# Last residual groups, three statistics groups and the gathered copies of the first phase moved into the next step's first slot

## The reference, cut to what matters

```python
x = x + L0_conv(_ln_c(x), ...)       # clustering mixer, below
t = t + L0_ffn(_ln_t(t), ...)        # per token, 96 -> 384 -> 96, values rounded to fp8 e5m2 / f16
x = x + L1_conv(_ln_c(x), ...)       # depthwise 3x3, 1x5, 5x1, then 1x1, times x
t = t + L1_ffn(_ln_t(t), ...)
```

```python
centers = pool(feat)                                  # 4 centres, means over sub-quadrants
sim  = sigmoid(beta + alpha * cos(centers, feat))     # 4 numbers per token and head
sim  = sim * (one-hot of the first maximum)           # ties go to the first centre
agg  = (sim @ value + value_centers) / (sum(sim) + 1) # gather
out  = agg^T @ sim ;  y = proj(out)                   # spread back, residual added
```

## Time and profile before

| | |
|---|---|
| median of 3 runs | 3742.16 us |
| the profiled execution, its time | 3745.27 us |
| the same, span of its trace | 3743.4 us |
| DVE busy | 3187.9 us (85%) |
| PE busy | 2901.5 us (78%) |
| ACT busy | 2795.3 us (75%) |
| POOL busy | 1723.0 us (46%) |
| `phase_a` | from 0 to about 2055 us |

### The profile page before, as it was taken

One profiled execution on the slowest core, in us unless ns is written; L12 is line 12 of the kernel. 1 busy time (PEld: TensorE's weight loads), 2 busy tenths in 40 slices (PEclk: granted clock), 3 DMA queues, 4 the chain that ended last, 5 costly groups with the idle time before them and its releaser, 6 DMA issues. The chain is left out here.

```text
span 3743.4 us, 65658 instructions
## 1 busy us (share of the span) xinstructions
PE 2901.5 (78%) x20710; PEld 1901.6 (51%) x20710; DVE 3187.9 (85%) x8131; ACT 2795.3 (75%) x6274; POOL 1723.0 (46%) x2404
## 2 busy tenths in 40 slices
PE   5777777777777777677766899996878888887877
PEld 5565556555565656565643344442444444444443
DVE  4888888888888888888886799998888889889887
ACT  2577777777777777777778455553999999999998
POOL 3777777777777777777764000000222222222221
PEclk7788888888889888988887899998999999999999
DMA  3232323232323232323222888896666666666661
GB/s 66 52 79 76 86 74 89 69 86 69 86 69 86 69 86 69 86 69 85 69 60 75 222 236 237 238 295 178 183 175 175 195 174 178 191 178 174 189 189 57
DMA packets 696169, 478.77 MB, mean 128 GB/s; under 512 B 407217, under 2 KB 674422, under 8 KB 683830
## 3 DMA queue, kind: packets, MB, share of 16 engines
q1 hardware_dynamic: 695830, 474.58, 48.0%
HBM read 272.09 MB, written 201.92 MB: 127 GB/s over the span
## 5 line engine op out<-in xcount | busy, mean ns | idle before, releaser
L1881 POOL TENSOR_SCALAR C_var<-C_st 128x16 f32<-128x16 f32 x64 | 16.6, 259 | 1385.1 <-DVE C_st L178 1385.1
L1455 DVE SCALAR_TENSOR_TENSOR B_y<-B_mid,B_coefs,B_y 128x512 f32<-128x512 f32 x768 | 509.0, 742 | 3.2 <-ACT B_y L1420 3.2
L1386 PE MATMUL B_ps_row<-B_z,B_band 128*128 128x512 f32 x1152 | 497.6, 594 | 13.5 <-DMA B_band<-edge_scratch 13.5
L378 DVE TENSOR_SCALAR A_hq<-A_h,A_b 128x512 f16<-128x512 f16 x768 | 293.8, 418 | 236.4 <-ACT A_h L370 230.1
L370 ACT ACTIVATE A_h<-A_hid 128x512 f16<-128x512 f32 x768 | 427.1, 592 | 64.4 <-PE A_hid L357 61.4
L178 DVE BATCH_NORM_STATS2 A_st<-A_xT 128x6 f32<-128x192 f32 x1536 | 443.1, 349 | 26.2 <-ACT A_xT L852 13.0
L370 ACT ACTIVATE C_h<-C_hid 128x512 f16<-128x512 f32 x768 | 426.3, 592 | 16.7 <-PE C_hid L357 9.1
L1495 ACT ACTIVATE C_q<-C_xT,C_shift,C_rstd 128x96 fp8e5<-128x96 f32 x1024 | 391.5, 456 | 31.4 <-POOL C_shift L1888 31.4
L167 POOL TENSOR_TENSOR A_rstd<-A_var,A_expo 128x16 f32<-128x16 f32 x128 | 374.7, 2927 | 10.7
L885 ACT ACTIVATE A_xc<-A_xT,A_shift,A_rstd 128x96 f32<-128x96 f32 x1024 | 379.2, 456 | 0.0
L1386 PEld LDWEIGHTS B_ps_row<-B_z,B_band 128*128 128x128 f32 x1152 | 218.2, 190 | 291.5 <-issue 285.8
(11 more groups left out here) (165 smaller groups left out, 6985.2 us busy)
## 6 DMA issues: line engine op xcount, KB each, us to landing
A_xq<-in_x SPq DMA_DIRECT2D x32, 1536.0 KB, 8.9
x_scratch<-A_xT SPq DMA_DIRECT2D x64, 768.0 KB, 3.2
x_scratch<-A_x3h SPq DMA_DIRECT2D x64, 768.0 KB, 5.4
B_z<-x_scratch SPq DMA_DIRECT2D x96, 512.0 KB
y_scratch<-B_y SPq DMA_DIRECT2D x96, 512.0 KB, 3.6
C_x3q<-x_scratch SPq DMA_DIRECT2D x32, 1536.0 KB, 9.0
C_xT<-x_scratch SPq DMA_DIRECT2D x64, 768.0 KB, 15.5
C_y3q<-y_scratch SPq DMA_DIRECT2D x31, 1536.0 KB, 15.4
```

What stands on the lines that cost most here:

```text
L378: r = dve.tensor_scalar(self.hq[:, b, s], self.h16[:, b, s], self.w["b1"][:, j:j + 1], 0.0, ALU.add, ALU.max)
L1386: m = pe.matmul(bank(c, h), band[c.buf(NB)][:, d, :], z[c.buf(NB)][:, half(h), d:d + W], start=(d == 0), stop=(d == 2))
L1455: dve.scalar_tensor_tensor(y, mid[c.buf(2)][:, half(h), t:t + W], coefs[:, c.n, 3 + t:4 + t], y, ALU.mult, ALU.add).then_inc(ev["sums"], 1)
```

## The change

- `OUT_AT` keeps groups 0 to 5 in slots 3, 4, 5; groups 6 and 7 (`OUT_LATE`) go to slot 0 of the next step, where the block is i itself. POOL's `ln2(·, 1)` goes with them: it now stands near the head of the next step's POOL queue, as `ln2(i, 1)`.
- `bn1` of q4 has its own tables: groups 0, 1 in slot 7, 2, 3, 4 in slot 8, and 5, 6, 7 in slot 0 of the next step (`BN1_AT`, `BN1_LATE`). `fwd` stays. The residual groups' statistics are issued before `bn1`, and `similarity` before both.
- `gather_out` goes from slot 8 to slot 0 of the next step, behind the hidden work. `own_heads` goes to the start of slot 2, `values` to the end of slot 1.
- `turn_sim` goes from slots 5 and 7 to 6 and 8; the centres' chain (`SIDE_AT` to `CN2_AT`) one slot later, `CW_AT` stays 8.
- PE issues the late `out(i, i, k)` in slot 0 behind both `big` groups and ahead of `sum_rows`. The list of bank uses follows, so the uses four entries apart are others: `agg` now comes four after `fwd` of group 5, and `out(6)` four after `agg`.
- POOL's queue is reordered: see the end of the diff.
- `similarity` writes its masks into a wider `eq` (9 floats per token and head) and no longer copies mask 0; `projected` is one `scalar_tensor_tensor` with a constant block mask instead of four `tensor_scalar`.

In the diff, the order of calls that is changed stands first for PE, then for DVE (from `ff.dve_hidden` on), last for POOL (`body`).

```diff
-OUT_AT = {3: (0, 1), 4: (2, 3), 5: (4, 5), 6: (6, 7)}
+OUT_AT, OUT_LATE = {3: (0, 1), 4: (2, 3), 5: (4, 5)}, {0: (6, 7)}
+BN1_AT, BN1_LATE = {7: (0, 1), 8: (2, 3, 4)}, {0: (5, 6, 7)}
-SIMT_AT = {5: 0, 7: 1}
-SIDE_AT, STD_AT, MEAN_AT, CF_AT, CN2_AT, CW_AT = 2, 2, 3, 4, 5, 8
-AGG_AT, SUM_AT, VAL_AT, PA_AT = 8, 0, 1, 2
+SIMT_AT = {6: 0, 8: 1}
+SIDE_AT, STD_AT, MEAN_AT, CF_AT, CN2_AT, CW_AT = 3, 3, 4, 5, 6, 8
+AGG_AT, GATHER_AT, SUM_AT, VAL_AT, HEADS_AT, PA_AT = 8, 0, 0, 1, 2, 2
...
             if s == AGG_AT:
-                front_uses.append(("agg", 0, 2, "gathered", 0))
+                front_uses.append(("agg", 0, 2, "gathered", 1))
...
+                    for k in OUT_LATE.get(s, ()):
+                        if i.real:
+                            out(i, i, k)
...
-                e = eq[:, u, :]
+                e = eq[:, u, 0:M]
...
-                dve.tensor_copy(taken[:, u, 0], e[:, :, 0]).then_inc(ev["tie"], 1)
...
-                for t in range(TPC):
-                    g = slice(32 * t, 32 * t + 32)
-                    m = dve.tensor_scalar(pabd[g, t * C:(t + 1) * C], s_pa[g, 0:C], rden[g, :], None, ALU.mult)
-                m.then_inc(ev["pabd"], 1)
+                dve.scalar_tensor_tensor(pabd[:].rearrange("p (t c) -> p t c", c=C),
+                                         s_pa[:, 0:C].unsqueeze(1).to_broadcast([P, TPC, C]), rden[:],
+                                         own_block.unsqueeze(2).to_broadcast([P, TPC, C]),
+                                         ALU.mult, ALU.mult).then_inc(ev["pabd"], 1)
...
                         ff.dve_hidden(dve, i, s)
+                    if q1.real and s == GATHER_AT:
+                        gather_out(q1)
                     for c in BIG_AT.get(s, ()):
                         if q2.real:
                             norms(q2, c)
...
+                    for k in OUT_LATE.get(s, ()):
+                        if i.real:
+                            x1(i, k)
                     for k in OUT_AT.get(s, ()):
                         if q1.real:
                             x1(q1, k)
-                    for k in FWD_AT.get(s, ()):
-                        if q4.real:
-                            bn(q4, k, "xT", "bn1", st1)
+                    if q2.real and s in SIM_AT:
+                        similarity(q2, SIM_AT[s])
+                    for k in OUT_LATE.get(s, ()):
+                        if i.real:
+                            bn(i, k, "x1", "bn2", ff.st)
                     for k in OUT_AT.get(s, ()):
                         if q1.real:
                             bn(q1, k, "x1", "bn2", ff.st)
+                    for k in BN1_AT.get(s, ()):
+                        if q4.real:
+                            bn(q4, k, "xT", "bn1", st1)
+                    for k in BN1_LATE.get(s, ()):
+                        if q3.real:
+                            bn(q3, k, "xT", "bn1", st1)
...
             def body(i):
                 q1, q2, q3, q4, p = i + 1, i + 2, i + 3, i + 4, i - 1
+                if p.real:
+                    ln3(p, 1)
+                if i.real:
+                    ln2(i, 1)
+                    ff.pool_norm(pool, i, 2)
                 if q3.real:
                     ln1(q3, 1)
                     r_by_side(q3, 1)
...
+                if q2.real:
+                    inverse_norms(q2, 0)
+
+                    pool.wait_ge(ev["rn"], ev.at("rn", q2, 0))
                 if i.real:
-                    ff.pool_norm(pool, i, 2)
...
+                    ff.pool_norm(pool, i, 3)
+                if q2.real:
+                    inverse_norms(q2, 1)
+
+                    pool.wait_ge(ev["rn"], ev.at("rn", q2, 1))
                 if i.real:
                     ln3(i, 0)
                 if q2.real:
                     scaled_sim(q2, 0)
                 if q1.real:
                     ln2(q1, 0)
+                    ff.pool_norm(pool, q1, 0)
                 if q3.real:
                     centres(q3)
-                if q1.real:
-                    ff.pool_norm(pool, q1, 0)
                 if q2.real:
                     scaled_sim(q2, 1)
                 if q1.real:
-                    ln2(q1, 1)
                     ff.pool_norm(pool, q1, 1)
```

More of the change, by code:

```diff
@@ L53 @@
 K_QUARTERS = K_ROWS + HM
-K_W = K_QUARTERS + M
+K_BLOCK = K_QUARTERS + M
+K_W = K_BLOCK + TPC
 class Events:
@@ L449, in phase_a @@
             back_uses += [("c", k, 0, "cout", k) for k in C_AT.get(s, ())]
-            if s == VAL_AT:
-                front_uses.append(("val", 0, 1, "aT4", 0))
             front_uses += [("big", c, 2, "big", c) for c in BIG_AT.get(s, ())]
+            front_uses += [("out", k, 0, "x1", k) for k in OUT_LATE.get(s, ())]
             front_uses += [("out", k, 1, "x1", k) for k in OUT_AT.get(s, ())]
@@ L471, in phase_a @@
                     c16=1, cw=1, cwc=1, big=NK, n2=NK, n2c=2, seed=2, rn_s=22, rn=2, guarded=2, cos=2, sig=2, mx=2, eq=2,
-                    tie=6, only=2, sim=2, simr=2, simT=2, side=1, sided=1, pool=1, agg=1, gathered=2, sum=1, summed=1, val=1,
+                    tie=2 * (M - 2), only=2, sim=2, simr=2, simT=2, side=1, sided=1, pool=1, agg=1, gathered=2, sum=1, summed=1, val=1,
                     rden=1, aT4=1, pa=1, pabd=1, bn3=NK,
@@ L763, in centre, with out @@
                 pe.matmul(out, lhs, rhs, start=True, stop=True).then_inc(ev[stage], 1)
-            def out(i, k):
-                q = i + 1
+            def out(i, q, k):
                 if k == 0:
@@ L806, in body @@
                         ff.pe_y(pe, i, s - 1)
+                    for k in OUT_LATE.get(s, ()):
+                        if i.real:
+                            out(i, i, k)
                     for k in OUT_AT.get(s, ()):
                         if q1.real:
-                            out(i, k)
+                            out(i, q1, k)
                     for k in FWD_AT.get(s, ()):
@@ L814, in body @@
                         sum_rows(i)
+                    if q1.real and s == VAL_AT:
+                        values(i)
                     if q1.real and s == PA_AT:
@@ L1115, in body @@
                 for s in range(FFN_SLOTS):
-                    if q1.real and s == VAL_AT:
+                    if q1.real and s == HEADS_AT:
                         own_heads(q1)
@@ L1139, in body @@
                             bn(q1, k, "x1", "bn2", ff.st)
+                    for k in BN1_AT.get(s, ()):
[4 more added lines that the diff above has]
+                            bn(q3, k, "xT", "bn1", st1)
                     if q1.real and s == PA_AT:
                         projected(q1)
-                    if q2.real and s in SIM_AT:
-                        similarity(q2, SIM_AT[s])
-                    if q2.real and s == AGG_AT:
-                        gather_out(q2)
                     if q1.real and s == SUM_AT:
@@ L1255, in body @@
                     r_by_side(q3, 1)
+                if q2.real:
+                    inverse_norms(q2, 0)
+                    pool.wait_ge(ev["rn"], ev.at("rn", q2, 0))
                 if i.real:
-                    ff.pool_norm(pool, i, 2)
-                if p.real:
-                    ln3(p, 1)
-                for h in range(2):
-                    if q2.real:
-                        inverse_norms(q2, h)
-                        pool.wait_ge(ev["rn"], ev.at("rn", q2, h))
-                    if i.real and h == 0:
-                        ff.pool_norm(pool, i, 3)
+                    ff.pool_norm(pool, i, 3)
+                if q2.real:
+                    inverse_norms(q2, 1)
+                    pool.wait_ge(ev["rn"], ev.at("rn", q2, 1))
                 if i.real:
@@ L1935 @@
         consts[32 * t:32 * t + M, K_QUARTERS:K_QUARTERS + M] = np.eye(M, dtype=np.float32) / np.float32(2 * CH)
+    for t in range(TPC):
+        consts[32 * t:32 * t + 32, K_BLOCK + t] = 1
     consts[0:C, K_CEN:K_CEN + C] = np.eye(C, dtype=np.float32) - np.float32(1 / C)
```

22 lines of the change are left out of this document (12 added, 10 removed).

## The result

| | before | after |
|---|---|---|
| median of 4 runs | 3742.43 us (3741.0 to 3745.09) | 3851.23 us (3850.41 to 3853.87) |
| span of the profiled execution | 3743.4 us | 3849.4 us |
| DVE busy | 3187.9 us | 3250.5 us |
| PE busy, mean clock | 2901.5 us, 0.90 | 3012.7 us, 0.87 |

The change makes the kernel slower: ratio 1.0289, 95% interval 1.0276 to 1.0302. The forecast was 3762 us with a range to 3806; the sign was right, the size was not.

A forecast was written before the change was run, and what follows sets the result against it. A chain that changes engines sets the step, no engine being full: 23.1 + 28.7 + 10.6 = 62.4 us against 61.43, +25 over 28 steps, -5 after. +20 on 3745.3 gives 3765, median 3762 us, range 3695 to 3806.

The forecast's parts named there:

- T to C: From DVE's first hidden work in slot 0 to its `cosines(0)` in slot 3: 23.1 us against 19.3, through POOL's queue.
- C to h: From DVE's `cosines(0)` to the end of slot 7's hidden work: 28.7 us against 33.01, DVE taken as bound.
- h to T: From DVE's slot 7 hidden work ending to the next step's first: 10.6 us against 9.0, gather behind ACT's copy.
- 28 steps: The steady steps of `phase_a`, each +0.9 us longer: +25 us in all.
- the rest: Pipeline fill 0; steps 29 to 31, with less on POOL and more room on DVE, -5 us.
- Rival A: PE at the low clock for the late `out`, `bn2` 1.5 us later: +42, 3804 us, chance 0.17.
- The rule on the clock: PE idling is followed by 1.2 GHz: two `out` groups take 2.93 us, not 1.46; the sum used the full level.
- Rival B: The gather stays hidden, 9.0 us from slot 7's hidden work to the next step: 60.7 a step, 3717 us, chance 0.20.
- C (no wait at `cosines(0)`): DVE reaches `cosines(0)` 19.4 us into the step without waiting for POOL: 58.6 us a step, 3657 us, chance 0.08.

The follow-up runs named there:

- the experiment with the two savings: The kernel before with only the cheaper `similarity` and the fused `projected`, nothing moved: 3747.05 us, ratio 1.0008.
- both edits: The changed kernel with `turn_sim(1)` back in slot 7 and POOL's `ln1(q3, 1)` and `r_by_side` behind `inverse_norms(q2, 0)`: 3755.03 us, ratio 1.0025.
- the fastest: The changed kernel with `turn_sim(1)` in slot 7, `ln1(q3, 1)` behind `inverse_norms(q2, 0)`, and `gather_out` ahead of slot 0's hidden work: 3719.02 us, ratio 0.9936.

## Why the prediction was right in sign and wrong in size

Its own terms, in us, against what most steps of the profiled execution show:

| | predicted | measured |
|---|---|---|
| T to C | 23.1 | 23.10 (24.5 at the low clock) |
| C to h | 28.7 | 30.0 |
| h to T | 10.6 | 11.75 (10.5 when the low clock is elsewhere) |
| 28 steps | +25 | +93 |
| the rest: fill, last steps, later phases | -5 | +13 |

**T to C was right, with its parts.** `out(6)` started at T + 4.0 (said: about 3.95) behind 1.67 us of idling (said 1.5); POOL took the late statistics at T + 7.3 (said 7.3), and `cosines(0)` waited 3.4 us (said 3.7) for a POOL queue of 15.8 us. The kernel with POOL's order changed shows it as the cause: without 3.8 us of that queue T to C is 20.0.

**C to h is the first step that failed: "28.7 us" subtracted removed work from a stretch in which the rest was taken as fixed.** It measured 30.0. These differences make up the missing 1.3 us. The three chunks of slot 3 took 2.58 us, 1.44 in the kernel before: +1.1. One L383 took 1.06 instead of 0.56: +0.5. Slot 4's hidden work and the add behind it took 0.2 more, the masks, 9 floats apart, 0.06 a half (0.42 against 0.36), the second `cosines` 0.1. The chunks of slot 7 and the tiny square of `cf` gave back some 0.7. The largest is POOL's doing. `cosines(0)` and `pool_norm(i, 3)` both follow the end of `inverse_norms(0)`, so they start at once (994.11 and 994.15), and the 3.5 us of `pool_norm` cover the three chunks from 995.23 to 997.81 nearly whole. Before, DVE came 1.6 us later than that end, and `pool_norm` was over 0.8 us into them. The kernel with the later `pool_norm` has 0.87 us there, so the contention is 1.7 us of the 2.58. The Trainium skill, "SBUF — State Buffer", section "Who interferes with whom", says that a DVE instruction in a 2-port mode, which `tensor_scalar` can enter, and a GpSimd one block each other whole, whichever issues first having the shared ports. The times agree with it; in which mode the three ran, no row shows. C to h didn't shrink when this contention was gone, so it isn't shown that 28.7 would have been reached without it. A second chain over PE and ACT is close behind DVE, as the experiment with the two savings shows, and the prediction had no term for it.

**h to T, the second, had the right mechanism and one term mis-sized: the gather, 1.64 us in the sum, measured 2.79.** The gather did move behind the copy of group 5; where it ran at 2.4 GHz the stretch was 10.5 us, as said (10.6). In most steps the gather ran at 1.2 GHz, 1.26 us longer, and the stretch was 11.75. I had used one gather of the kernel before, at 919.16 us. Its trace has the other price as well, in two of the steps 1 to 27, and h to T is 10.15 us in these instead of 9.0:

```profile
796.33 2.79 PE L712 MATMUL A_fbank<-A_xT,A_simr 128*32 128x96 f32 x64
```

**The clock was put into one rival, at one place.** Rival A priced it at the late `out` (+1.5, 24.6 in all; measured 24.2 to 24.5 where it fell there). It fell at the gather in 20 of 28 steps and at `out` in 5, so it was paid in 25. In the changed kernel both places are on the chain. The kernel with extra matmuls took it from the gather and got it at `out`, with the same 64.8 us.

**The rule on the clock, that idling is followed by the low level, doesn't hold as the prediction used it.** The idling just in front doesn't decide. PE in the changed kernel, three stretches:

```profile
909.89 2.93 PE L774 MATMUL A_fbank<-A_pabd,A_simT 128*128 128x384 f32 x4 [1.67 <-DVE A_gathered L1060]
...
1090.26 2.15 PE L678 MATMUL A_fbank<-A_cst,A_xq 96*128 96x96 f32 x12
1092.20 1.06 PE L704 MATMUL A_fbank<-A_cst,A_sim 128*128 128x128 f32 x4
1094.37 2.79 PE L715 MATMUL A_fbank<-A_xT,A_simr 128*32 128x96 f32 x64 [1.10 <-ACT A_xT L857]
```

The `out` at 909.89 is at the low level and the one at 974.89, shown above, at the full one, both behind 1.67 us; so the argument against rival A, that 1.5 us is less than 2.15, had nothing to stand on. The gather at 1094.37 is low behind 1.10 us and the one at 965.48 full behind 1.13. In front of both, `fwd` and `turn_sim(1)` were at the low level already (granted clock 0.50 from 1089.3 to 1093.3 us, 0.53 from 960.4 to 964.4): at the gather the low stretch begins before the gap, and the question is whether it ends in time. In two kernels the gather is low with no gap in front, the one with both edits and the fastest. The late `out` was low only behind its gap: without it, in the two kernels with the early `gather_out`, in none of 56 steps. With POOL's order changed both gaps stay (1.3 to 1.4 and 1.67 us), and in 21 of 28 steps both groups are at the full clock. So a gap is neither enough for the low level nor always needed. What sets the moment at which the level changes was not tested, and no run held the clock fixed. Why the step comes to 64.8 in four different kernels (the changed one, the extra matmuls, the later `pool_norm`, the early `gather_out` alone) is open as well: it may be chance, or a closed loop between the length of the step and the clock.

**Of the whole miss**, 86 us on the profiled execution (3851.25 against 3765 forecast), C to h makes 1.3 x 28 = 36, h to T 1.15 x 28 = 32 (with the steps that paid at `out` instead), and the rest 18 (13 where -5 was said). Of the 13, 4.6 lie in front of step 0, 5.6 in the last steps of `phase_a` and the others behind it; their causes are open. In the kernels above step 0 starts anywhere from 117 to 136 us.

Rival B (gather hidden) and C (no wait at `cosines(0)`) didn't come true in this kernel, yet an edit brings each about or nearly (h to T 9.57, a wait of 0.33), and with both and the early copy the change's idea is worth 23 us instead of costing 109.

## What to carry to other kernels

Work moved to a later slot can cost nothing where the engine idles, but every queue it is moved past has to be summed up to its next consumer: here moving 3.8 us of POOL work from in front of `inverse_norms` made the kernel 87 us faster, and its order was free to choose. When matmuls lie on the chain, price them at both clocks, wherever they stand, and read the level from many steps and not from one: the trace before had both prices of the gather. A stretch in which an engine has hardly a gap need not be bound by that engine alone: look how close the next chain follows, since it can take what is saved.

## What the runs showed of the hardware

- Three 128x512 f16 DVE instructions took 0.87 us alone, 1.44 with POOL's `pool_norm` over their first 0.8 us, and 2.58 with it over nearly all of them. A 128x384 f16 add took 0.35 us alone and 2.38 in the worst place, once in every step. DVE and POOL of the changed kernel there, slot 8:

```profile
1025.03 1.69 DVE L179 BATCH_NORM_STATS2 A_st<-A_xT 128x6 f32<-128x192 f32 x6
1026.65 2.38 DVE L250 TENSOR_TENSOR A_y16b<-A_y,A_b 128x384 f16<-128x384 f16 x1
...
1029.65 2.22 DVE L179 BATCH_NORM_STATS2 A_st<-A_xT 128x6 f32<-128x192 f32 x8
```

```profile
1025.62 1.62 POOL L221 TENSOR_TENSOR A_xc<-A_xT,A_st 128x384 f32<-128x384 f32 x2
1027.20 1.61 POOL L230 TENSOR_TENSOR A_q<-A_xc,A_rstd 128x384 fp8e5<-128x384 f32 x2
```

- The add ends 0.2 us after POOL's last instruction does (1028.81). The statistics are not touched: 0.28 us each with POOL working (six in 1.69) and without (eight in 2.22).
- Adding eight matmuls of no use cost nothing in the total time (3853.0 against 3851.2) and brought nothing: PE's low stretch moved from the gather to the late `out`, 9.4 us on, in most steps.
- The same four `out` matmuls behind the same 1.67 us of idling took 1.56 us in the step of 974.89 of the changed kernel and 2.93 in that of 909.89; 23 of 28 steps had the first.
